# Layer 0's experts: three PSUM banks for the inner products, and gate, product, down product and copy a step or two later

## The chip, the cores and the metric

One NeuronCore of a Trainium2 chip runs the whole program. The metric is the device time of one execution in microseconds, as the median of several runs. Beside it there is one execution taken with the hardware profiler; its trace is where all rows below come from. The engines are called PE (TensorE, the matmuls), ACT (ScalarE), DVE (VectorE), POOL (GpSimd) and SP (SyncE, here only a DMA queue).

## The reference, cut to what matters

Two layers, each with cross attention and then a mixture of experts, on 32 sequences of 128 tokens of 128 features. The change touches the experts of layer 0:

```
# x: 4096 tokens (32 x 128) of 128 features, after a layer norm; 8 experts, the best 2 a token
scores = x @ Wr.T + br                       # 8 a token
idx    = top_k(scores + biases, 2);  val = softmax(scores)[idx], scaled to sum 1
h      = x @ Wl1[n] + bl1[n]                 # 128 -> 512 = a (256) and b (256)
y_n    = (silu(a) * b) @ Wl2[n] + bl2[n]     # 256 -> 128
x      = x + tanh(g_ffn[0]) * sum over the two experts of val * y_n
```

Layer 1 follows with its own attention (16 heads of 8) and experts (gelu, no gate product).

## The kernel before, in words

The whole program is one list of tasks, the plan, made by `order()` from generators that yield one step at a time. Each engine walks the same list and runs its own part of each task in that order; semaphores join the engines. So the plan's order is each engine's queue order, and a task that waits holds all that stands behind it on its engine.

For the experts the tokens are first routed: each token's row is scattered by POOL into a table in DRAM, sorted by expert, and the table is cut into blocks of 128 rows of one expert. Layer 0 has 71 blocks. `expert_steps` (L299) yields their steps. Of a block i, with the place of its tasks in the plan as it was:

- `fetch`: SP loads the block's 128 rows from DRAM, ten steps ahead.
- `turn` (step i): PE transposes the rows (L1160); ACT copies the transpose to `xb` (L1366) and copies half of the expert's weights to a ring, `block_w` (L1373); DVE computes where the results go (L1723) and copies the other half of the weights (L1735).
- `up` (step i+2): PE makes four 128x128 products into one PSUM bank (L1171); two parts are a, two are b. A product has eight records in the trace. The banks alternate, `UP_BANK` 0 and 1, so product i waits for `hidden` of block i-2. In the same task ACT makes `gate` = silu(a + bias) (L1383).
- `hide` (step i+2): DVE makes `hidden` = (b + bias) * gate (L1743), which reads the bank for the last time.
- `down` (step i+4): PE multiplies `hidden` by the second weights (L1191) into one of two other banks, and waits for the copy of block i-2 out of it. In the same task DVE adds a bias and copies the result to `y_sb` (L1758).
- `store` (step i+4): POOL scatters the 128 result rows to DRAM by an indirect DMA (L1925).

`xb` has 4 buffers, `block_w` 4, `gate` 2, `hidden` 3, `y_sb` 6. Between these tasks stand the routing of the last token group, the tables of the second part of the blocks, POOL's clears (L1871), the first keys of layer 1 (`k1`, `k_load`), and, from step 53 on, `load` and `combine`: ACT issues the load of a sequence's two results a token (L1395), and DVE adds them to `x` (L1767). `k1`, `q1` and `xt` use PSUM bank 5 (`SPLIT_BANK`), the routing of layer 0 and the bias tables bank 7 (`ROUTE_BANK`). Layer 1's attention starts in the plan at step `BLOCKS[0] + 2` of this stage, and its scores (L993) use banks 0 and 1.

Of the kernel before, what the change touches and what calls it, by code (L numbers as in the profile page):

```python
# [18 lines left out]
ACT = mybir.ActivationFunctionType  # L19
# [46 lines left out]
SPLIT_BANK = 5  # L66
UP_BANK = (0, 1)
X_BANK = (3, 2)
Y_BANK = (4, 6)
# [229 lines left out]
def expert_steps(layer, tasks, begun, after):  # L299
# [11 lines left out]
    for b in range(AMONG[layer]):  # L311
        begins = FIRST_DONE[layer] + 6 + (4 * b // 3 if layer == 0 else 11 * b // 10)
        loads.setdefault(begins, []).append(("load", layer, b))
        combines.setdefault(begins + 3, []).append(("combine", layer, b))
    begin_after = max(combines) - len(after)
    if layer == 0:
        begin_after = min(s for s in combines if ("combine", 0, GS - 1) in combines[s]) - after.index([("norm", NG)])
    for s in range(max(max(combines) + 1, n_blocks + 4)):
        step = []
        if 0 <= s - 2 < n_blocks:  # L320
            step.append(("up", first + s - 2))
# [5 lines left out]
        if s < n_blocks:  # L327
            step.append(("turn", first + s))
        if layer == 0 and 0 <= s - 2 < n_blocks:
            step.append(("hide", s - 2))  # L330
        if 0 <= s - 4 < n_blocks:
            step += [("down", first + s - 4), ("store", first + s - 4)]
        if rest:
# [23 lines left out]
def order():  # L357
# [8 lines left out]
    after0 = [[("expert", 1, e)] for e in range(NEXP)] + first_keys_and_queries()  # L366
    phases = [(attention0_steps(tasks[0]), NSEQ), (expert_steps(0, tasks[0], NSEQ + 4, after0), BLOCKS[0] + 2),
              (attention1_steps(tasks[1]), U1 + 1), (expert_steps(1, tasks[1], U1 + 5, []), BLOCKS[1])]
# [20 lines left out]
def flamingo_two_layers(nc, a, out):  # L389
# [31 lines left out]
    def xt_count(n):  # L421
        return place["xt", n] + 1
# [45 lines left out]
    with ExitStack() as stack:  # L468
# [253 lines left out]
        def blocks_of_tile(layer, b):  # L722

            return FIRST_BLOCK[layer] + (FIRST_DONE[layer] if b < GS * FIRST_GROUPS[layer] else BLOCKS[layer])

        def hiddens(n):

            return n + min(max(n, 0), BLOCKS[0])
# [181 lines left out]
        def _(pe):  # L910
            w = Waits(pe)

            def three_pass(to, wh, wl, xh, xl):
                pe.matmul(to, wh, xh, start=True, stop=False)  # L914
                pe.matmul(to, wl, xh, start=False, stop=False)
                return pe.matmul(to, wh, xl, start=False, stop=True)

            def split_task(t):
# [36 lines left out]
                elif t[0] == "q1":  # L955
                    n = NG + t[1]
                    w.wait_ge("weights1", 6)
                    w.wait_ge("split_lo", xt_count(n))
                    done = three_pass(banks[:, bank, :], w1_h[:, 0, :], w1_l[:, 0, :], xt_h[:, n % 2, :], xt_l[:, n % 2, :])
                else:  # L960
                    c0 = t[1] * GK
                    w.wait_ge("weights1", 6)
                    done = three_pass(banks[:, bank, 0:GK], w1_h[:, 1, :], w1_l[:, 1, :],
                                      ctx_th[:, c0:c0 + GK], ctx_tl[:, c0:c0 + GK])
# [81 lines left out]
            for t in plan:  # L1046
# [114 lines left out]
                elif kind == "up":  # L1161
# [5 lines left out]
                    w.wait_ge("shifted", NSEQ + layer * U1)  # L1167
                    w.wait_ge("hidden", hiddens(i - 1))
                    w.wait_ge("xb", i + 1)
                    for part in range(4 if layer == 0 else 2):  # L1170
                        done = pe.matmul(banks[:, UP_BANK[i % 2], part * P:(part + 1) * P], block_w[:, i % WR, part // 2, part % 2 * P:(part % 2 + 1) * P], xb[:, i % BR, :],  # L1171
                                         start=True, stop=True)
# [56 lines left out]
        def _(act):  # L1229
# [12 lines left out]
            for t in plan:  # L1242
# [118 lines left out]
                elif kind == "turn":  # L1361
# [5 lines left out]
                    if i < BLOCKS[0]:  # L1367
# [6 lines left out]
                                       ACT.Copy).then_inc(sem("block_w_act"))  # L1374
                elif kind == "up":
                    i = t[1]
                    layer, k, n = of_block(i)
                    w.wait_ge("up", i + 1)
                    if layer == 0:
                        w.wait_ge("hidden", hiddens(i - 1))  # L1380
                        w.wait_ge("block_bias", k + 1)
                        for half in (0, 1):
                            act.activation(gate[:, i % 2, half, :], banks[:, UP_BANK[i % 2], half * P:(half + 1) * P], ACT.Silu,  # L1383
                                           bias=block_bias[:, k, half, n:n + 1]).then_inc(sem("gate"))
                    else:
                        w.wait_ge("y_mm", i - HR + 1)
                        act.activation(hidden[:, i % HR, :, :].rearrange("p t n -> p (t n)"), banks[:, UP_BANK[i % 2], 0:HID1], ACT.Gelu).then_inc(sem("hidden"))  # L1387

# [31 lines left out]
        def _(dve):  # L1420
# [14 lines left out]
            for t in plan:  # L1435
# [300 lines left out]
                elif kind == "hide":  # L1736
# [5 lines left out]
                    for half in (0, 1):  # L1742
                        dve.scalar_tensor_tensor(hidden[:, i % HR, half, :], banks[:, UP_BANK[i % 2], (2 + half) * P:(3 + half) * P],  # L1743
                                                 block_bias[:, k, 2 + half, n:n + 1], gate[:, i % 2, half, :], ALU.add, ALU.mult).then_inc(sem("hidden"))
                elif kind == "down":
                    i = t[1]
# [208 lines left out]
```

## Time and profile before

| | us |
|---|---|
| median of 3 runs | 788.54 |
| lowest and highest | 787.5, 790.2 |
| the profiled execution's own time | 795.85 |
| its span | 794.1 |

The span runs from the first to the last instruction of the program; the execution's own time has some more around it. The profiled execution is 0.9% above the median. The products of layer 0's experts run from 247.5 to about 412 us of the span. "Idle before" in a row is time in which the engine did nothing before these instructions, and the name behind the arrow is what ended it. PE's ends are modelled, its starts are not.

### The profile page before, as it was taken

To read this page: it belongs to the slowest core of one execution; us is meant where nothing else is said; L and a number is where in the kernel's file an instruction comes from. 1 tells how busy PE (TensorE), PEld (TensorE's weight loads), DVE (VectorE), ACT (ScalarE), POOL (GpSimd) and SP (SyncE) were. 2 spreads that over 40 slices of the span, in tenths; PEclk is the share of its full clock that TensorE was granted. 3 is DMA by queue.
4 is the path that set the end of the run, shared out by engine and by line. 5 is a ranking of instruction groups with operands and counts; after the bars stand their busy time and mean duration, and the time that the engine had idled before them with its cause. 6 is when DMAs were issued, how large, how long until landed. Compare 5 with 4: busy or idle time off the path is not lost.

```text
span 794.1 us, 16522 instructions
## 1 busy us (share of the span) xinstructions
PE 647.0 (81%) x4501; PEld 584.0 (74%) x4501; DVE 556.0 (70%) x1971; ACT 442.0 (56%) x1275; POOL 448.4 (56%) x665
## 2 busy tenths in 40 slices
PE   6888888899766767978688899889879875898886
PEld 5677778888666657877677788878768874787775
DVE  3367688887874566876787889888878755444564
ACT  2476767677434434655556776767665542433452
POOL 4035357776667565875445334767656665565541
PEclk9999999998978788999997999999999996999999
DMA  9446667454422223434352435535413013332444
GB/s 261 117 115 171 174 172 182 124 154 110 127 72 87 62 79 113 110 93 119 106 156 76 114 78 107 122 85 103 113 58 84 31 34 93 102 89 79 135 145 153
DMA packets 127383, 89.48 MB, mean 113 GB/s; under 512 B 30996, under 2 KB 116276, under 8 KB 127260
## 3 DMA queue, kind: packets, MB, share of 16 engines
q1 hardware_dynamic: 110844, 64.93, 32.1%
q0 software_dynamic: 8128, 17.65, 6.8%
q10 hardware_dynamic: 8320, 5.85, 2.6%
q8 instruction: 38, 0.62, 0.3%
q14 instruction: 53, 0.43, 0.2%
HBM read 50.73 MB, written 39.85 MB: 114 GB/s over the span
## 4 chain that ended last, share of the span: by engine, by line
PE 39%; DVE 21%; issue 12%; ACT 11%; SPq 5%; another core or an unknown queue 4%; DMA 3%; POOL 2%; DVEq 1%; ACTq 0%; POOLq 0%
PE banks L1171 7%; PE banks L1191 5%; PE banks L1034 5%; SPq L824 3%; DMA v_rows<-vo 3%; DVE row_max L1428 3%; PE banks L914 2%; PE banks L1001 2%; PE banks L977 2%; PE banks L1212 2%; PE banks L1019 2%; DVE hidden L1743 2%; DVE up L1735 2%; DVE x_res L1767 2%
## 5 line engine op out<-in xcount | busy, mean ns | idle before, releaser
L1925 POOL DMA_INDIRECT y_rows<-y_sb,result_at x134 | 131.1, 978 | 107.9 <-DVE result_at L1723 46.5
L1171 PE MATMUL banks<-xb,up 128*128 128x128 f32 x820 | 127.8, 297 | 47.1 <-DVE hidden L1743 22.4
L1171 PEld LDWEIGHTS banks<-xb,up 128*128 128x128 f32 x820 | 112.8, 207 | 61.5 <-issue 33.7
L1918 POOL DMA_INDIRECT x_rows<-xm,row x120 | 120.5, 1004 | 31.6 <-issue 28.5
L1880 POOL TENSOR_TENSOR v_flat<-v_raw,row_head 104x64 f32<-104x64 f32 (+1 forms) x128 | 55.6, 461 | 73.1 <-ACT v_raw L1345 72.1
L1191 PE MATMUL banks<-down,hidden 128*128 x536 | 87.6, 289 | 8.9 <-DVE y_sb L1760 4.6
L1329 ACT ACTIVATE prob_t<-banks 128x512 f32<-128x512 f32 x192 | 73.3, 439 | 28.7 <-PE banks L1001 24.8
L1034 PE MATMUL banks<-v_flat,prob_t 128*128 128x108 f32 (+2 forms) x640 | 86.5, 284 | 3.3 <-ACT prob_t L1329 1.3
L1034 PEld LDWEIGHTS banks<-v_flat,prob_t 128*128 128x128 f32 (+1 forms) x640 | 79.7, 197 | 10.6 <-ACT prob_t L1329 6.8
L1383 ACT ACTIVATE gate<-banks,block_bias 128x128 f32<-128x128 f32 x142 | 44.4, 365 | 76.2 <-PE banks L1171 44.7
L1191 PEld LDWEIGHTS banks<-down,hidden 128*128 128x128 f32 x536 | 75.0, 202 | 12.0 <-issue 12.0
L1846 POOL TENSOR_TENSOR prob<-prob,inv_sum 128x616 f32<-128x616 f32 x32 | 39.1, 1223 | 57.8 <-DVE inv_sum L1491 57.6
L1743 DVE SCALAR_TENSOR_TENSOR hidden<-banks,block_bias,gate 128x128 f32<-128x128 f32 x142 | 42.8, 343 | 33.8 <-ACT gate L1383 27.5
L1428 DVE TENSOR_REDUCE row_max<-banks 128x8 f32<-128x616 f32 x64 | 50.4, 788 | 9.3 <-PE banks L993 9.3
L1001 PE MATMUL banks<-ident,prob 128*128 128x128 f32 (+1 forms) x375 | 56.3, 283 | 0.0
L1019 PE MATMUL banks<-vo_flat,prob_t 128*128 128x128 f32 (+1 forms) x320 | 47.4, 302 | 8.6 <-ACT prob_t L1329 6.6
L1735 DVE COPY up<-up 128x256 f32 x134 | 49.5, 370 | 6.9 <-issue 2.4
L1019 PEld LDWEIGHTS banks<-vo_flat,prob_t 128*128 128x128 f32 (+1 forms) x320 | 45.2, 217 | 9.7 <-ACT prob_t L1329 7.4
L1387 ACT ACTIVATE hidden<-banks 128x256 f32<-128x256 f32 x63 | 24.0, 382 | 45.9 <-PE banks L1171 35.8
L1760 DVE COPY y_sb<-banks 128x128 f32<-128x128 f32 x63 | 18.1, 287 | 44.5 <-PE banks L1191 32.3
L1304 ACT ACTIVATE prob<-banks,row_max 128x77 f32<-128x77 f32 x128 | 30.8, 324 | 32.7 <-issue 20.4
L1001 PEld LDWEIGHTS banks<-ident,prob 128*128 128x128 f32 (+1 forms) x375 | 46.2, 147 | 0.8 <-issue 0.2
(238 smaller groups left out, 1657.9 us busy)
## 6 DMA issues: line engine op xcount, KB each, us to landing
vo_flat<-v_rows SPq DMA_DIRECT2D x32, 256.0 KB
x_norm<-x_rows SPq DMA_DIRECT2D x74, 72.0 KB
v_rows<-vo SPq DMA_DIRECT2D x38, 128.0 KB
x_far<-x_rows SPq DMA_DIRECT2D x60, 72.0 KB
gathered<-y_rows ACTq DMA_DIRECT2D x32, 128.0 KB
q_rows<-up_raw SPq DMA_DIRECT2D x8, 512.0 KB, 2.8
q_even<-q_rows SPq DMA_DIRECT2D x12, 256.0 KB
q_odd<-q_rows SPq DMA_DIRECT2D x12, 256.0 KB
```

Of the source, the lines that this page charges most:

```text
L1001: done = pe.transpose(banks[0:chunk_rows[c], PT_BANK[k], c % 4 * SEQ:(c % 4 + 1) * SEQ], flat[:, c * P:c * P + chunk_rows[c]], ident[:, :])
L1019: done = pe.matmul(banks[:, O_BANK, 0:D], prob_t[0:rows, b % 2, c, :], vo_flat[0:rows, b % 2, c, :], start=c == 0, stop=c == CHUNKS - 1)
L1034: done = pe.matmul(banks[:, O_BANK, half * width:half * width + cols], prob_t[0:rows, u % 2, c, :], v1_flat[0:rows, first:first + cols], s ...
L1171: done = pe.matmul(banks[:, UP_BANK[i % 2], part * P:(part + 1) * P], block_w[:, i % WR, part // 2, part % 2 * P:(part % 2 + 1) * P], xb[: ...
L1191: done = pe.matmul(banks[:, Y_BANK[i % 2], 0:D], hidden[:, i % HR, half, :], of_expert(flat[:, (2 * layer + half) * D:], i, D), start=half ...
L1329: act.activation(dst, banks[0:rows, PT_BANK[k], 0:len(chunks) * SEQ], ACT.Copy).then_inc(sem("prob_t"))
L1428: dve.tensor_reduce(m_view, s_view, AX.X, ALU.max).then_inc(sem("row_max"))
L1735: dve.tensor_copy(block_w[:, i % WR, 1 - layer, :], src[:, bass.ds(at, HID1)]).then_inc(sem("block_w_dve"))
L1743: dve.scalar_tensor_tensor(hidden[:, i % HR, half, :], banks[:, UP_BANK[i % 2], (2 + half) * P:(3 + half) * P], block_bias[:, k, 2 + half, ...
L1880: pool.tensor_tensor(v1_rows[0:rows, b % 2, half, chunks[0]:chunks[-1] + 1, :, 0:DK1], v1_raw[0:rows, chunks[0]:chunks[-1] + 1, half, :, : ...
L1918: pool.indirect_dma_start(out=x_rows[layer][:, :], out_offset=bass.IndirectOffsetOnAxis(ap=row[:, n, c:c + 1], axis=0), in_=xm[:, i % 2, j ...
L1925: pool.indirect_dma_start(out=y_rows[layer][:, :], out_offset=bass.IndirectOffsetOnAxis(ap=result_at[:, i % (2 * YR):i % (2 * YR) + 1], ax ...
```

## The change

Layer 0's products go round three banks, 0, 1 and a third that is bank 5 before block 28 and bank 7 from there on. Each product waits for the last reader of its own bank. The gate gets a task of its own and stands at step i+3, ahead of that step's other tasks; `hide` stands at step i+3 (it was i+2), the down product at step i+5 (i+4), and DVE's copy, now a task `keep`, and the store at step i+6 (i+4). Loads, combines and the work of the next phase stand two steps later; the stage has two more steps of its own. The experts of layer 1 keep their order.

```diff
+UP_SWITCH = 28
-        begins = FIRST_DONE[layer] + 6 + (4 * b // 3 if layer == 0 else 11 * b // 10)
+        begins = FIRST_DONE[layer] + (8 + 4 * b // 3 if layer == 0 else 6 + 11 * b // 10)
-    for s in range(max(max(combines) + 1, n_blocks + 4)):
+    for s in range(max(max(combines) + 1, n_blocks + 6 - 2 * layer)):
         step = []
+        if layer == 0 and 0 <= s - 3 < n_blocks:
+            step.append(("gate", s - 3))
         if 0 <= s - 2 < n_blocks:
             step.append(("up", first + s - 2))
...
-        if layer == 0 and 0 <= s - 2 < n_blocks:
-            step.append(("hide", s - 2))
-        if 0 <= s - 4 < n_blocks:
-            step += [("down", first + s - 4), ("store", first + s - 4)]
+        if layer == 0:
+            if 0 <= s - 3 < n_blocks:
+                step.append(("hide", s - 3))
+            if 0 <= s - 5 < n_blocks:
+                step.append(("down", s - 5))
+            if 0 <= s - 6 < n_blocks:
+                step += [("keep", s - 6), ("store", s - 6)]
+        elif 0 <= s - 4 < n_blocks:
+            step += [("down", first + s - 4), ("keep", first + s - 4), ("store", first + s - 4)]
...
-    phases = [(attention0_steps(tasks[0]), NSEQ), (expert_steps(0, tasks[0], NSEQ + 4, after0), BLOCKS[0] + 2),
+    phases = [(attention0_steps(tasks[0]), NSEQ), (expert_steps(0, tasks[0], NSEQ + 4, after0), BLOCKS[0] + 4),
...
+        def up_bank(i):
+            if i >= BLOCKS[0]:
+                return UP_BANK[i % 2]
+            return (UP_BANK[0], UP_BANK[1], SPLIT_BANK if i < UP_SWITCH else ROUTE_BANK)[i % 3]
+        def up_before(i):
+            first = 0 if i < BLOCKS[0] else BLOCKS[0]
+            return max([j for j in range(first, i) if up_bank(j) == up_bank(i)], default=first - 1)
...
+                    w.wait_ge("hidden", 2 * UP_SWITCH)      # PE, task k1
...
-                    w.wait_ge("hidden", hiddens(i - 1))     # PE, task up
+                    w.wait_ge("hidden", hiddens(up_before(i) + 1))
+                    if up_bank(i) == SPLIT_BANK:
+                        w.wait_ge("split_lo", xt_count(NG - 1))
+                    elif up_bank(i) == ROUTE_BANK:
+                        w.wait_ge("block_bias", 2)
...
-                elif kind == "up":                          # ACT
+                elif kind == "gate":
...
-                elif kind == "down":                        # DVE
+                elif kind == "keep":
```

## Rows read from the trace of the kernel before

**Rows 1.** The page: span, busy time by engine, TensorE's granted clock in tenths.

```profile
span 794.1 us, 16522 instructions
...
PE 647.0 (81%) x4501; PEld 584.0 (74%) x4501; DVE 556.0 (70%) x1971; ACT 442.0 (56%) x1275; POOL 448.4 (56%) x665
...
PEclk9999999998978788999997999999999996999999
```

**Rows 2.** Stretches of the stage: busy us (instructions) of each engine, clock, DMA.

```profile
262.00:316.00 54.00, 39.39 (x261) 37.22 (x260) 33.45 (x147) 21.30 (x78) 29.54 (x33) 0.79 0.29 84
316.00:350.00 34.00, 29.69 (x246) 28.33 (x245) 28.08 (x91) 19.89 (x73) 27.30 (x31) 0.99 0.37 103
350.00:395.00 45.00, 32.69 (x270) 30.78 (x269) 30.58 (x125) 24.13 (x89) 22.82 (x24) 1.00 0.42 115
395.00:413.00 18.00, 16.70 (x122) 15.42 (x120) 15.34 (x58) 10.36 (x35) 8.58 (x9) 0.91 0.52 147
sum 151.00, PE 118.48 PEld 111.75 DVE 107.45 ACT 75.68 POOL 88.25; mean PE 29.62 PEld 27.94 DVE 26.86 ACT 18.92 POOL 22.06
```

**Rows 3.** Waits in 262 to 415 us: engine, line, releaser: us, times, longest.

```profile
ACT gate L1383 <- PE banks L1171: 44.7, 37, 3.4
...
PE banks L1171 <- DVE hidden L1743: 21.3, 18, 5.6
PEld banks L1171 <- ACT up L1373: 17.8, 10, 5.8
ACT gate L1383 <- remote: 13.5, 2, 8.3
...
PE banks L1191 <- DVE y_sb L1758: 4.0, 3, 1.8
```

**Rows 4.** Groups in 262 to 415 us: busy us, mean ns, idle before.

```profile
L1171 PE MATMUL banks<-xb,up 128*128 128x128 f32 x526 | 77.4, 294 | 24.9 <-DVE hidden L1743 21.3 <-issue 1.9 <-DVE up L1735 0.9
```

**Rows 5.** Timeline at full pace: start us, us, engine, line (PE only).

```profile
317.16 1.06 PE L1171 MATMUL banks<-xb,up 128*128 128x128 f32 x8
...
318.17 0.61 PE L1191 MATMUL banks<-down,hidden 128*128 x4
...
318.61 1.06 PE L1171 MATMUL banks<-xb,up 128*128 128x128 f32 x8
```

**Rows 6.** Timeline of a pause, 352 to 357 us, columns as above.

```profile
352.30 1.13 PE L1171 MATMUL banks<-xb,up 128*128 128x128 f32 x8 [0.80 <-DVE hidden L1743]
...
353.83 1.06 PE L1171 MATMUL banks<-xb,up 128*128 128x128 f32 x8
...
355.56 0.62 ACT L1383 ACTIVATE gate<-banks,block_bias 128x128 f32<-128x128 f32 x2 [2.69 <-PE banks L1171]
...
356.07 0.28 ACT L1366 ACTIVATE xb<-banks 128x128 f32<-128x128 f32 x1
356.21 0.61 DVE L1743 SCALAR_TENSOR_TENSOR hidden<-banks,block_bias,gate 128x128 f32<-128x128 f32 x2 [2.27 <-ACT gate L1383]
356.23 0.42 ACT L1373 ACTIVATE up<-up 128x256 f32 x1
...
356.53 0.63 ACT L1383 ACTIVATE gate<-banks,block_bias 128x128 f32<-128x128 f32 x2
356.75 0.29 DVE L1758 TENSOR_TENSOR y_sb<-banks,down_bias 128x128 f32<-128x128 f32 x1
...
357.08 1.13 PE L1171 MATMUL banks<-xb,up 128*128 128x128 f32 x8 [1.22 <-DVE hidden L1743]
```

**Rows 7.** Timeline of the longest hold.

```profile
288.74 0.96 POOL L1918 DMA_INDIRECT x_rows<-xm,row  x1 [0.30 <-issue]
291.30 0.62 ACT L1383 ACTIVATE gate<-banks,block_bias 128x128 f32<-128x128 f32 x2 [8.29 <-remote]
```

**Rows 8.** Timeline at the stage's end, a combine on DVE.

```profile
413.08 0.73 DVE L1767 SCALAR_TENSOR_TENSOR x_res<-gathered,token_w,x_res 128x128 f32<-128x128 f32 x2
```

**Rows 9.** Timeline early in the stage, a product at half clock.

```profile
267.40 2.05 PE L1171 MATMUL banks<-xb,up 128*128 128x128 f32 x8
```

More of the change, by code:

```diff
@@ L1167, in _ @@
                     w.wait_ge("shifted", NSEQ + layer * U1)
-                    w.wait_ge("hidden", hiddens(i - 1))
+                    w.wait_ge("hidden", hiddens(up_before(i) + 1))
[3 more added lines that the diff above has]
+                        w.wait_ge("block_bias", 2)
                     w.wait_ge("xb", i + 1)
                     for part in range(4 if layer == 0 else 2):
-                        done = pe.matmul(banks[:, UP_BANK[i % 2], part * P:(part + 1) * P], block_w[:, i % WR, part // 2, part % 2 * P:(part % 2 + 1) * P], xb[:, i % BR, :],
+                        done = pe.matmul(banks[:, up_bank(i), part * P:(part + 1) * P], block_w[:, i % WR, part // 2, part % 2 * P:(part % 2 + 1) * P], xb[:, i % BR, :],
                                          start=True, stop=True)
@@ L1374, in _ @@
                                        ACT.Copy).then_inc(sem("block_w_act"))
-                elif kind == "up":
+                elif kind == "gate":
                     i = t[1]
-                    layer, k, n = of_block(i)
+                    _, k, n = of_block(i)
                     w.wait_ge("up", i + 1)
[L1379 to L1387, printed above, removed]
+                    w.wait_ge("hidden", hiddens(i - 1))
+                    w.wait_ge("block_bias", k + 1)
+                    for half in (0, 1):
+                        act.activation(gate[:, i % 2, half, :], banks[:, up_bank(i), half * P:(half + 1) * P], ACT.Silu,
+                                       bias=block_bias[:, k, half, n:n + 1]).then_inc(sem("gate"))
+                elif kind == "up" and t[1] >= BLOCKS[0]:
+                    i = t[1]
+                    w.wait_ge("up", i + 1)
+                    w.wait_ge("y_mm", i - HR + 1)
+                    act.activation(hidden[:, i % HR, :, :].rearrange("p t n -> p (t n)"), banks[:, up_bank(i), 0:HID1], ACT.Gelu).then_inc(sem("hidden"))
                 elif kind == "load" and t[2] < AMONG[t[1]]:
@@ L1742, in _ @@
                     for half in (0, 1):
-                        dve.scalar_tensor_tensor(hidden[:, i % HR, half, :], banks[:, UP_BANK[i % 2], (2 + half) * P:(3 + half) * P],
+                        dve.scalar_tensor_tensor(hidden[:, i % HR, half, :], banks[:, up_bank(i), (2 + half) * P:(3 + half) * P],
                                                  block_bias[:, k, 2 + half, n:n + 1], gate[:, i % 2, half, :], ALU.add, ALU.mult).then_inc(sem("hidden"))
-                elif kind == "down":
+                elif kind == "keep":
                     i = t[1]
```

## The prediction

> **What bounds the kernel now.** I read the page first. TensorE (PE) is busy for 81% of the span, more than any other engine, and no engine is full [rows 1]. The change touches one stage, the experts of layer 0, so I cut it out by stretches: from 262 to 413 us PE's matmuls are busy for 118.5 of 151 us, DVE 107.5, POOL 88.3, ACT 75.7 [rows 2]. The reader is to see that PE has 32.5 us of idle time there and that it is uneven: 14.6 us in 262 to 316, 4.3 in 316 to 350, 12.3 in 350 to 395, 1.3 in 395 to 413.
>
> The waits of that stage say what the idle time is [rows 3]. PE's inner products (L1171) wait 18 times for DVE's `hidden` (21.3 us), and the load of their weights 10 times for ACT's copy of them (17.8 us); these are the same pauses, seen from two sides, so I don't add them. ACT's gates in turn wait 37 times for those very matmuls, 44.7 us. It is a ring: product of block i, gate i, hidden i, product of block i+2 in the same bank.
>
> How fast the ring could turn is seen where it is undisturbed: a block's product starts at 317.16 and the next at 318.61, so PE needs 1.45 us a block, and the down product starts 1.01 us after the product [rows 5]. Over the stage it is 2.3 us a block: 526 records of a product, eight to a block, are 66 blocks in 262 to 415 us [rows 4]. Where the rest goes is seen in one pause [rows 6]. PE records a product from 352.30 to 353.43, but its gate starts only at 355.56, 2.1 us later; the following product ended at 354.89 and its gate is the very next one. ACT was idle for 2.69 us, "<- PE". So PE's signals reach the others late and several at once. From the gate's start (call it R) the ring takes 0.65 us to `hidden` (356.21), 0.61 for that pair, and 0.26 to PE's next product at 357.08: R + 1.52. The largest such hold is 8.29 us, until 291.30; POOL's last scatter before it had ended at 289.70 [rows 7]. That is a coincidence in time, not a shown cause.
>
> **The change part by part.** It adds and removes no arithmetic: the same matmuls, gates, `hidden`, copies and stores, 71 of each. It moves them.
>
> Banks. Product i waits for `hidden` of block i-3, no longer i-2. By itself this takes `hidden` out of the ring in which PE now waits: there are three steps for it, 4.35 us at full pace.
>
> Gate and `hidden` a step later. In ACT's queue the order of a step was gate(s-2), transposed rows xb(s), weights(s); it becomes gate(s-3), xb(s), weights(s). After a hold the gate in front is now an old one, already done, so at R ACT starts with xb. In [rows 6] xb starts 0.51 after the gate and the weights 0.16 after xb, 0.42 long. Without the 0.51, weights are ready at 0.16 + 0.42 = 0.58, and PE follows at 0.58 + 0.26 = R + 0.84 in place of R + 1.52: 0.68 us saved a pause at best. This ring (transpose s, xb, weights, product s) still spans only two steps; it is what is late next.
>
> Down product and copy. Down(s-5) stands in step s and needs its bank's copy y(s-7), which `keep` makes in DVE's step s-1. Before, two steps lay between that copy and its bank's next use; now one. After a hold, xb and weights come first, the next gate starts 0.46 us later (356.53 after 356.07 [rows 6]), `hidden` 0.65 after that, the copy 0.54 after `hidden` and 0.29 long, and 0.26 to PE: R + 2.20. PE, restarted at R + 0.84, arrives there at + 1.01 = R + 1.85 and waits 0.35. So the net saving is 0.68 - 0.35 = 0.33 at worst in this arithmetic, 0.68 where the copy was early. I take 0.5, the middle. Also `hidden` of i needs down(i-3) out of its buffer; that now sits right behind product i, 0.6 us, about as long as the gate takes, so it costs 0 to 0.1 a block and is hidden by the gate.
>
> Sum: 18 pauses [rows 3] x 0.5 = 9.0 us saved. Bounds: 18 x 0.33 = 5.9, and above it all of PE's idle time.
>
> Ends. Layer 0's loads and combines, the work that comes along from the next phase (key and query loads, clears, k1), and the start of layer 1's attention all stand two steps later, with the blocks where they were. The two added steps have no product; DVE does two copies (0.29) and a combine (0.73) more between the last `hidden` and layer 1's first scores [rows 6, 8]: 1.3 us, I take 1.5 with the gather that ACT issues; 0 to 3 as bounds. The wait that k1's split now has on `hidden` of block 27 stands six steps behind it in the plan: 0. Products in bank 7 from block 28 on wait for the second bias table, copied at step 23: 0. SP's fetches keep their steps, ten blocks ahead: 0. POOL's stores come one step later on the plan (two steps after the first blocks), its queue is otherwise the same; from 316 to 350 it is busy 27.3 of 34 us with 31 instructions [rows 2], near full with the time between two issues, so nothing can be gained there, and almost nothing is lost there now (4.3 us of PE idle).
>
> Total: -9.0 + 1.5 = -7.5. The profiled execution's own time is 795.85 us (span 794.1), 0.9% above the median of 788.54; I take the difference off the median: **781.0 us**.
>
> **Two rules beside the rows.** The row says that a gate starts 2.1 us after its matmul's recorded end [rows 6]. The Trainium skill, page "Perfetto Trace Analysis", section "Tensor Engine Instruction (MATMUL, LD_WEIGHTS)", says that TensorE's end in a profile is estimated from the instruction's size, and that its semaphore is pushed once PSUM has acknowledged. By that the products could truly be running in those 2 us; then PE has nothing to give and the sum is rival C, 790, not 781.
>
> On the clock the stage is granted 1.00 from 350 to 395, although PE pauses most often there, and 0.79 from 262 to 316 [rows 2]. The skill's page "TensorE: Matmul & The Clock Gate", section "A second HAM failure mode: psum-queue depth-cycling", speaks against this change: cycling through PSUM banks gave PE small pauses between groups, in which the clock swung between its two levels. By that the time would be rival E's.
>
> **The rivals.**
> B, the pauses go almost wholly. For it: three blocks in flight cover 2 us of hold at 1.45 a block. Against: the xb ring keeps two steps. Of the 32.5 us of PE idle [rows 2] I leave 5.6, the pause behind the 8.29 us hold, and some 2: -25, plus 1.5: 765.
> C, nothing comes of it: PE is truly busy during the holds, or the holds are tied to POOL's stores, and a quicker restart only brings the next one earlier. For it: the longest hold ends behind a scatter of POOL [rows 7]. Against: at 317 the ring runs at 1.45 us [rows 5] in a stretch in which POOL, with its stores, is near full [rows 2]. Cost: the ends only, +1.5: 790.
> D, slower: the down product takes over the wait. The trace has three such waits now, 4.0 us, 1.33 each [rows 3], with two steps of slack. With one step, each block whose copy stands behind combines (0.73 each) or routing on DVE meets it: some 34 blocks in 262 to 316 and 395 to 413, a third of them at 1.33 = 15, less the 9 won, plus 1.5: +7.5, 796. It decides from the point where DVE's copy ends later than 1.01 us after the next product starts. For it: DVE is busy 15.3 of 18 us from 395 to 413 [rows 2]. Against: there PE's idle is 1.3 us at present.
> E, the clock: at 1.2 GHz the eight records of a product take 2.05 us, not 1.06 [rows 9], and a block some 1.45 more. Eight more blocks in such windows are +11.6: 800.
>
> **How the numbers follow.** Chances: forecast 0.47, B 0.17, C 0.17, D 0.14, E 0.05. The forecast's own range is 774 to 786: 2 to 15 us gained. The range of 8 in 10 reaches into B and over C: 765 to 794. A measurement tells about 0.3% (2.4 us) from no change. Faster by more: forecast and B, 0.64. Within it: C, 0.17. Slower by more: D and E, 0.19.
>
> **What would show it.** In the profile after: 350 to 395's blocks about 0.2 us shorter each; fewer and shorter waits of L1171 on `hidden`, and the remaining ones named on ACT's copy of the weights or xb; gates no longer idle for 44.7 us on PE, since they come a step later; waits of the down product on `y_sb` up from 4.0 us, but under 9. If those exceed 15 us, D holds. If PE's idle in the stage stays at 30 us with the holds as long, C. If it is under 12 us, B. Wrong altogether if the time moves in a stage that the change does not touch.

## The result and the profile after

The change makes the kernel slower: 797.48 us (median of 4 runs, 796.77 to 801.36) against 789.37 (787.5 to 793.14) on the same chip, a ratio of 1.0100 with the 95% interval [1.0062, 1.0138]. The forecast was 781.0, with a range up to 794. Repeated on a chip on which the kernel before takes 794 us, the ratio was 1.0134 [1.0100, 1.0167]; on one on which it takes 744.6 us, 1.0072 [1.0039, 1.0104].

The profiled execution of the changed kernel took 797.59 us, about its median. The one of before took 795.85, 0.9% above its own median, so the two spans can't be subtracted; I compare what happens inside the stage, and leave the totals to the timed runs.

From the page of the changed kernel, answering to [rows 1]:

```profile
span 795.8 us, 16588 instructions
...
PE 655.7 (82%) x4501; PEld 588.0 (74%) x4501; DVE 555.3 (70%) x1971; ACT 447.9 (56%) x1275; POOL 448.0 (56%) x665
...
PEclk9999999999868887999997999999999996799999
```

The stretches of the stage, answering to [rows 2]:

```profile
262.00:316.00 54.00, 40.64 (x263) 38.20 (x264) 32.17 (x147) 22.17 (x77) 28.23 (x31) 0.78 0.26 76
316.00:350.00 34.00, 29.62 (x223) 27.17 (x222) 25.56 (x86) 19.90 (x68) 24.99 (x28) 0.95 0.38 106
350.00:395.00 45.00, 38.08 (x289) 34.75 (x287) 31.48 (x126) 26.30 (x90) 23.92 (x26) 0.96 0.41 110
395.00:413.00 18.00, 14.91 (x109) 13.02 (x110) 15.04 (x56) 11.58 (x37) 8.30 (x10) 1.00 0.51 139
```

And the waits in 262 to 415 us, answering to [rows 3], with the two groups of PE that answer to [rows 4]. "Remote" stands where the profile names no instruction of this core as what ended the wait:

```profile
ACT xb L1390 <- PE banks L1180: 31.3, 24, 4.0
DVE hidden L1768 <- ACT gate L1406: 28.5, 14, 6.0
...
ACT xb L1390 <- remote: 20.2, 4, 6.8
PE banks L1215 <- DVE y_sb L1783: 17.3, 14, 4.4
...
PEld banks L1195 <- ACT up L1397: 10.3, 8, 2.4
...
PE banks L1195 <- ACT up L1397: 8.5, 5, 2.2
```

```profile
L1195 PE MATMUL banks<-xb,up 128*128 128x128 f32 x520 | 77.9, 297 | 12.8 <-ACT up L1397 8.5 <-issue 3.9
L1215 PE MATMUL banks<-down,hidden 128*128 x267 | 47.4, 304 | 17.8 <-DVE y_sb L1783 17.3 <-issue 0.2
```

L1195 is the inner product, L1215 the down product, L1180 the transpose, L1783 the copy of y. The reader is to see three things. The wait that the change aimed at is gone: the inner product's idle time fell from 24.9 us [rows 4] to 12.8, and none of it is put down to `hidden`. In its place stands a wait that was 4.0 us, three times [rows 3]: the down product waits 14 times, 17.3 us, for DVE's copy out of its bank. And ACT, which waited for inner products at its gates, now waits for transposes at its copies (31.3 and 20.2 us). Records of inner products in 262 to 415 us went from 526 to 520: the stage does not run faster. From 262 to 413 us PE is idle for 27.8 us instead of 32.5, and busy for 123.3 instead of 118.5 with slightly fewer instructions (884 for 899), so the smaller idle time is not a gain.

One such place in the timeline (start us, us, engine, line; idle before in brackets):

```profile
282.67 1.13 PE L1195 MATMUL banks<-xb,up 128*128 128x128 f32 x8
...
286.07 0.61 DVE L1768 SCALAR_TENSOR_TENSOR hidden<-banks,block_bias,gate 128x128 f32<-128x128 f32 x2 [3.77 <-remote]
286.60 0.28 DVE L1783 TENSOR_TENSOR y_sb<-banks,down_bias 128x128 f32<-128x128 f32 x1
...
287.02 1.22 PE L1215 MATMUL banks<-down,hidden 128*128 x4 [3.11 <-DVE y_sb L1783]
```

DVE's product (`hidden`) is held until 286.07. The copy is queued behind it on DVE and starts 0.53 us later; PE's down product, whose bank that copy empties, has waited 3.11 us for it. Before, that bank's copy stood one step further ahead. The three longest waits of this kind, 4.37, 3.11 and 3.18 us (down products at 262.80, 287.02 and 301.45), make 10.7 of the 17.3 us, and in each the copy starts 0.53 us behind a `hidden` that had been held for 3.8 to 6.0 us.

The same wait sits at the end of the stage, where PE goes over to layer 1's first scores (L1013):

```profile
412.12 1.13 PE L1195 MATMUL banks<-xb,up 128*128 128x128 f32 x8
413.08 0.61 PE L1215 MATMUL banks<-down,hidden 128*128 x4
414.62 0.71 PE L1215 MATMUL banks<-down,hidden 128*128 x4 [0.93 <-DVE y_sb L1783]
416.17 1.42 PE L1215 MATMUL banks<-down,hidden 128*128 x8 [0.84 <-DVE y_sb L1783]
417.34 0.53 PE L1013 MATMUL banks<-k_even,q_even 96*128 96x308 f32 x2
```

and in the kernel before:

```profile
410.52 1.13 PE L1171 MATMUL banks<-xb,up 128*128 128x128 f32 x8 [0.20 <-DVE hidden L1743]
411.48 1.29 PE L1191 MATMUL banks<-down,hidden 128*128 x8
413.10 0.52 PE L993 MATMUL banks<-k_even,q_even 96*128 96x308 f32 x2 [0.32 <-DVE hidden L1743]
```

From the start of the last inner product to the first scores: 2.58 us before, 5.22 after, 2.64 more.

### The profile page after: what moved, and what is told of

It is laid out like the page before. It is cut to its first block, busy times and chain, and to the rows that moved or that the text cites. A ratio compares the mean times of both kernels' runs of the same rounds, so it can differ in the third digit from the quotient of the medians.

```text
span 795.8 us, 16588 instructions
## 1 busy us (share of the span) xinstructions
PE 655.7 (82%) x4501; PEld 588.0 (74%) x4501; DVE 555.3 (70%) x1971; ACT 447.9 (56%) x1275; POOL 448.0 (56%) x665
## 4 chain that ended last, share of the span: by engine, by line
PE 36%; DVE 20%; issue 13%; ACT 12%; SPq 5%; DMA 4%; another core or an unknown queue 4%; POOL 4%; DVEq 1%; ACTq 0%; POOLq 0%
PE banks L1195 7%; PE banks L1215 5%; PE banks L1054 4%; SPq L843 3%; DVE row_max L1453 3%; DMA v_rows<-vo 2%; PE banks L933 2%; POOL y_rows L1950 2%; PE banks L1180 2%; PE banks L1021 2%; PE banks L997 2%; ACT prob L1328 1%; DVE prob L1456 1%; PE banks L1039 1%
## 5 line engine op out<-in xcount | busy, mean ns | idle before, releaser
L1195 PE MATMUL banks<-xb,up 128*128 128x128 f32 x820 | 129.5, 299 | 28.5 <-ACT up L1397 8.5
L1195 PEld LDWEIGHTS banks<-xb,up 128*128 128x128 f32 x820 | 114.4, 210 | 43.1 <-issue 22.2
L1215 PE MATMUL banks<-down,hidden 128*128 x536 | 92.6, 300 | 22.5 <-DVE y_sb L1783 18.1
L1215 PEld LDWEIGHTS banks<-down,hidden 128*128 128x128 f32 x536 | 77.6, 208 | 29.3 <-issue 29.1
L1390 ACT ACTIVATE xb<-banks 128x128 f32<-128x128 f32 x134 | 37.2, 278 | 72.0 <-PE banks L1180 40.6
L1785 DVE COPY y_sb<-banks 128x128 f32<-128x128 f32 x63 | 18.1, 287 | 42.4 <-PE banks L1215 26.4
```

The source lines that it names most:

```text
L1195: done = pe.matmul(banks[:, up_bank(i), part * P:(part + 1) * P], block_w[:, i % WR, part // 2, part % 2 * P:(part % 2 + 1) * P], xb[:, i ...
L1215: done = pe.matmul(banks[:, Y_BANK[i % 2], 0:D], hidden[:, i % HR, half, :], of_expert(flat[:, (2 * layer + half) * D:], i, D), start=half ...
```

## The experiments

Every ratio below is to the kernel before, on the chip of that run. "The stage" is the time in the profiled run from the end of block 0's inner product to the start of layer 1's first scores, read from the timeline. Four groups of runs came on four chips on which the kernel before takes 744 to 746 us, one group on a chip on which it takes 794. The first expectations give times for a chip with 789.4 us; only their ratios can be compared.

**The parts of the change, 744 us.** Three banks alone, every step as before (gate and product i + 2, down product and copy i + 4, tail as before):

```
-            step.append(("gate", s - 3))    # likewise hide
+            step.append(("gate", s - 2))
-                step.append(("down", s - 5))
+                step.append(("down", s - 4))
-                step += [("keep", s - 6), ("store", s - 6)]
+                step += [("keep", s - 4), ("store", s - 4)]
```

> Three PSUM banks for layer 0's products, but gate, hidden, down product, copy, store, loads and the next phase all at their old steps. Before is 789.4, the changed kernel 797.5. Theory D (the down product waits for a copy that stands one step before it instead of two): that wait stays near 4 us, the third bank costs nothing, 786 to 790. Rival T (the two steps of tail: later loads, combines and start of layer 1's attention cost the time): 787 to 790 as well, since the tail is the old one. Rival L (banks 5 and 7 themselves, or the gate's new place, cost): 793 or more if it is the banks.

Measured: 744.57 us, 1.0022 [0.9994, 1.0049]. Here the third bank by itself does nothing that can be told from zero. But this profile has no wait under "remote"; the third bank alone was not run on a chip with the late signals that it was meant to cover.

The same with the gate and product at i + 3:

```
-            step.append(("gate", s - 2))    # likewise hide
+            step.append(("gate", s - 3))
```

> Three banks, gate and hidden one step later, but down product, copy and store at step i+4 and the tail as before. Theory D: the copy keeps two steps of slack to the next use of its bank, so no gain is lost there; PE waits for hidden in the down product instead, one step behind it; 786 to 792. Rival T: 787 to 790. Rival L (the later gate costs by itself): 795 or more.

Measured: 749.00 us, 1.0059 [1.0030, 1.0088], above the kernel before, though its interval overlaps that of the third bank alone. What it adds is in its trace, 245 to 425 us: the down product, now one step behind `hidden` instead of two, waits for it.

```profile
PE banks L1215 <- DVE hidden L1768: 12.8, 14, 3.6
```

The change with the copy and the store in the down product's own step:

```
-            if 0 <= s - 6 < n_blocks:
-                step += [("keep", s - 6), ("store", s - 6)]
+            if 0 <= s - 5 < n_blocks:
+                step += [("keep", s - 5), ("store", s - 5)]
```

> The changed kernel with the copy out of the bank and the store at step i+5, beside the down product, instead of i+6; tail two steps later as in the change. Theory D: waits of the down product on y_sb fall from 18.1 us to under 6, and the time from 797.5 to 788 to 791. Rival T: the time stays at 795 to 798 though those waits are gone, since the tail is the changed kernel's.

Measured: 746.10 us, 1.0019 [0.9994, 1.0045], as theory D has it and not rival T; PE's wait for the copy is 2.0 us (3 times) from 245 to 425 us.

The change's order on two banks:

```
-            return (UP_BANK[0], UP_BANK[1], SPLIT_BANK if i < UP_SWITCH else ROUTE_BANK)[i % 3]
+            return UP_BANK[i % 2]
```

> The changed kernel's order (gate, hidden, down, copy, store and tail later) with the two old banks. Theory D: the third bank is what the later gate needs, without it PE waits for hidden of block i-2, now one step behind it: 800 to 806. Rival T: the banks don't matter, 797 to 799.

Measured: 766.73 us, 1.0319 [1.0290, 1.0348]; PE waits 21.5 us (22 times) for `hidden` from 245 to 390 us. The third bank is what the later gate needs, and on these chips it only pays that back.

**Repeats and two attempts at the order, 744 us.**

> The changed kernel as it is, on the chip of this call. The first four experiments ran where the kernel before took 744 us, not 789, and where no signal of PE came late. Theory D+H (the change adds the wait for the copy everywhere, and what it can win is only the cover of PE's late signals): where signals are prompt it is slower by more than 1%, about 1.015; where they are late about 1.010 again. Rival T (the tail of two steps): the same 1.010 on any chip.

> The kernel before as it is, for a second trace of it and for the noise: 0.998 to 1.002 of before. Where before takes 744 us every matmul's signal should follow its end within 0.1 us; where it takes 789 us gates of layer 0's experts should idle for 40 us and more again.

Measured: the change 749.00, 1.0072 [1.0039, 1.0104]; the kernel before against itself 1.0001 [0.9975, 1.0027], which is the error of the method. The change's loss is real on this chip too. Theory D+H had 1.015 here and is wrong in that: the loss is smaller where signals are prompt, not larger.

The copy put ahead of the product in DVE's step, still at i + 6:

```
-            if 0 <= s - 3 < n_blocks:
-                step.append(("hide", s - 3))
             ...
             if 0 <= s - 6 < n_blocks:
                 step += [("keep", s - 6), ("store", s - 6)]
+            if 0 <= s - 3 < n_blocks:
+                step.append(("hide", s - 3))
```

> The changed kernel, with one thing exchanged: in each step DVE copies the down product of six blocks ago out of its bank before it makes hidden, not after, so the copy no longer stands behind a gate. Theory D: PE's waits of the down product on y_sb fall from 18.1 us to under 5, and the time to 0.995 to 1.003 of before. Rival T: it stays within 0.2% of the changed kernel, as the tail is the same. Rival L (the later gate itself costs): the waits on y_sb go, but others take their place and it stays over 1.006.

Measured: 750.78, 1.0081 [1.0051, 1.0111]: nothing regained. I took this as evidence against the wait on the copy, but the wait did not go away with this order. From 245 to 425 us it is 9.5 us, against 6.7 (11 times) in the change on the same chip:

```profile
PE banks L1215 <- DVE y_sb L1783: 9.5, 16, 1.5
```

So this run does not test theory D. It also ran where no long hold stands, so what this order does to the waits of 3 to 4 us above is not known.

Gathers, combines and layer 1's first steps one step earlier:

```
-        begins = FIRST_DONE[layer] + (8 + 4 * b // 3 ...
+        begins = FIRST_DONE[layer] + (7 + 4 * b // 3 ...
-    ... expert_steps(0, tasks[0], NSEQ + 4, after0), BLOCKS[0] + 4)
+    ... expert_steps(0, tasks[0], NSEQ + 4, after0), BLOCKS[0] + 3)
```

> The changed kernel with loads, combines, the next phase's work and layer 1's attention one step earlier, so one step behind their old place and not two (two earlier would deadlock). Theory D: within 0.2% of the changed kernel. Rival T: half of the loss comes back, some 4 us.

Measured: 752.54, 1.0104 [1.0047, 1.0161], not better. Taking back one of the two added tail steps gains nothing.

**The start of the stage, 744 us.** In these profiles the first ten blocks (end of block 0's inner product to end of block 10's) took 19.4 us before and 23.0 in the change. ACT's timeline shows where. The kernel before (its repeat):

```profile
242.84 1.28 ACT L1383 ACT_TABLE_LOAD   x1
247.46 0.62 ACT L1383 ACTIVATE gate<-banks,block_bias 128x128 f32<-128x128 f32 x2 [3.33 <-PE banks L1171]
```

The change (its repeat):

```profile
248.01 0.28 ACT L1390 ACTIVATE xb<-banks 128x128 f32<-128x128 f32 x1 [4.87 <-PE banks L1180]
...
249.82 1.65 ACT L1321 ACTIVATE xm<-x_res,m_shift,m_rstd 128x128 f32<-128x128 f32 x4 [1.00 <-DVE m_shift L1558]
...
251.58 1.28 ACT L1406 ACT_TABLE_LOAD   x1
252.88 0.62 ACT L1406 ACTIVATE gate<-banks,block_bias 128x128 f32<-128x128 f32 x2
```

Gate 0, one step later, stands behind the last group's normalise (L1321), and the table load for Silu, which had filled ACT's wait for the first product, now stands in the way. First the load alone was moved back:

```
+                    if i == 1:
+                        act.activation(silu_first[:, :], zero[:, 0:1], ACT.Silu)
```

> The change, with one 128x1 Silu of a constant put behind the second block's weight copy on ACT, so that the table load for Silu (1.28 us, in the change right ahead of gate 0 at 251.58) lies in ACT's wait for the third transpose, as it did before. Theory S (the start: gate 0 came at 252.88 instead of 247.46, and the first ten blocks took 23.0 us instead of 19.4): if the load is what is late, the ratio to the kernel before falls from 1.007 by 1.3/744 to 1.005 and up 0 to up 10 takes 21.7 us. If the load only fills a wait that stands there anyway (for the normalise of the last group, 249.82), the ratio stays 1.007 and the ten blocks 23.0.

Measured: 749.25, 1.0037 [1.0016, 1.0057]; the first ten blocks took 20.1 us. The estimate is better than the change's 1.0072, but their intervals overlap.

Then the gates of the first ten blocks at their old step:

```
+        gates = [i for i in (s - 3, s - 2) if 0 <= i < n_blocks and (s - i == 2) == (i < EARLY)]
-            step.append(("gate", s - 3))    # likewise hide
+        step += [("gate", i) for i in gates]
```

> The change, but gate and product of blocks 0 to 9 stand at their old step (two steps behind the transpose's, ahead of the step's up product), those of the others a step later. Theory S (the loss of the start is the later gate behind the last group's normalise and the table load): up 0 to up 10 takes 19 to 20 us, the ratio falls from 1.007 to about 1.002. Rival (the start is slow because of the later down product and copies, or the loss only moves to blocks 10 to 20): the ten blocks take 21 us or more, or up 10 to up 34 takes 4 us more than 43, and the ratio stays at 1.006 to 1.008.

Measured: 750.95, 1.0078 [1.0045, 1.0110]. The ten blocks took 21.1 us, but the time is that of the change; where the rest went is not shown.

> The last one, and the copy and store of each block in the step of its down product (i + 5) instead of the step behind it, so that a down product waits for a copy of two steps ago. If both the start and the wait on the copy (theory D) are the loss, the gains add: 1.007 less 0.005 less 0.005 is 0.997, and the handover to layer 1's first scores is 0 to 1 us behind that of the kernel before instead of 3. If they are one loss seen twice, 1.002.

Its edit is the last one and that of the copy and store at i + 5. Measured: 744.21, 0.9973 [0.9952, 0.9994], the one kernel whose interval lies below its base. Against the run just above, on the same chip and with only the place of copy and store different, it gains 1.05% (7.8 us, 4.9 to 10.7 with both intervals); PE's wait for the copy falls from 6.7 us (12 times) to 1.5 (3 times), 245 to 425 us.

> The last one, with the gathers, the combines and layer 1's first steps one step earlier than in the change. If the two steps by which the change moves these cost time at the handover, this is 1 us (one step of 1.3 us) faster than the last, 0.996; if the gathers then wait for stores that have not landed, it is the same or 1 to 3 us slower, as it was for the change itself (1.010 against 1.007).

Its edit is the last one and the earlier tail. Measured: 747.87, 1.0004 [0.9978, 1.0030]. Its profile also shows how much one profile of the start is worth: the first blocks stand in the same order as in the last kernel and took 22.2 us, not 18.5.

**The copy or the store, 794 us.** Here the change had its full loss. The copy in its down product's step, the store left where the change has it, ten early gates:

```
+            if 0 <= s - 5 < n_blocks:
+                step.append(("keep", s - 5))
             if 0 <= s - 6 < n_blocks:
-                step += [("keep", s - 6), ("store", s - 6)]
+                step.append(("store", s - 6))
```

> Gates and products of blocks 0 to 9 at their old step, the rest a step later, every copy of y in the step of its down product (i + 5), but the store still a step later (i + 6). The kernel with copy and store both at i + 5 had the ratio 0.997, with both at i + 6 1.008. Theory D (what costs is that the next down product but one waits for the copy on DVE): the copy's place decides, 0.997 to 0.999. Rival (what costs is that the stores, and with them the gathers and y_sb's buffers, come a step later): the store's place decides, 1.005 to 1.008.

> The change itself, as the yardstick of this chip: 1.010 where the kernel before takes 789 us, 1.007 where it takes 744 us. On a chip of the first kind the three others, if the same two causes (the first blocks' gates, the copy's place) make the loss there too, stand 0.008 to 0.010 below it.

Measured: 793.53, 0.9990 [0.9963, 1.0017], against the change's 804.17, 1.0134 [1.0100, 1.0167]. The waits in 247 to 425 us of the change:

```profile
ACT xb L1390 <- PE banks L1180: 30.4, 22, 5.0
...
PE banks L1215 <- DVE y_sb L1783: 20.1, 16, 4.7
```

and with the copy at i + 5 (L1182 is the transpose, L1197 the inner and L1217 the down product, L1399 the weights' copy, L1785 the copy of y):

```profile
ACT xb L1392 <- PE banks L1182: 24.6, 22, 2.7
...
PEld banks L1197 <- ACT up L1399: 21.2, 13, 5.0
...
PE banks L1197 <- ACT up L1399: 16.5, 10, 4.8
DVE y_sb L1785 <- PE banks L1217: 12.5, 13, 1.7
```

PE's wait for the copy is down to 4.9 us (3 times); DVE now waits for the down product (12.5 us); the inner products' waits for `hidden`, which comes behind that on DVE, are 2.8 us (6 times). The stage took 160.6 us against 169.9 in both profiles of the change and 163.5 in that of before.

The gates at their old step for every block, down product, copy and store at i + 5:

```
-            step.append(("gate", s - 3))    # likewise hide
+            step.append(("gate", s - 2))
-                step += [("keep", s - 6), ("store", s - 6)]
+                step += [("keep", s - 5), ("store", s - 5)]
```

> Three banks, every gate and product of layer 0 at the old step (i + 2), down product, copy and store at i + 5: the change without its later gate and without its later copy. Against the kernel with ten early gates (0.997) it tells whether the later gate is worth anything once the first blocks are on. Theory G (a gate a step later takes 60 short waits of ACT for the product, 41 us of ACT's time, out of ACT's order, which then waits for the transposes instead, 14 to 24 us): the later gate has a small gain, this one has 1.000 to 1.002. Rival (the later gate gives nothing, the later down product with the copy in its step does it all): 0.997.

Measured: 796.36, 1.0038 [1.0013, 1.0064]; PE still waits 11.7 us (7 times) for the copy. The kernel above, with the gate later from block 10 on, had 0.9990: on this chip the later gate is worth 3.8 us (0.9 to 6.8 with both intervals), if the store's place is worth nothing.

> The kernel of ratio 0.997 (ten early gates, copy and store at i + 5) with the gathers, the combines and what hangs on them one step earlier, but layer 1's first steps where the change has them. With both earlier the ratio was 1.000. If the gathers are what collides (a gather queued on ACT before its stores have landed), this one has 1.000 as well; if it is layer 1's first steps, 0.997.

Its edit is that of the kernel of ratio 0.9973 and the first half of the tail's edit. Measured: 792.26, 0.9991 [0.9963, 1.0020]. No collision of the gathers is seen, and copy and store both at i + 5 do as well as the store a step later. As the gathers are moved too, this is no clean pair, but nothing points to the store's place as the cost.

**The copy alone, 744 us.** The edit is that of the kernel with ratio 0.9990 (`keep` at s - 5, `store` at s - 6), without its early gates:

> The change with the copy of y alone in its down product's step (i + 5), the store left at i + 6, the gates of all blocks a step later. The change had 1.0134 where the kernel before takes 794 us and 1.0072 where it takes 744; with this copy and ten early gates it had 0.999. Theory D (a down product waits for the copy, 20 us of PE's time in the change): this one takes most of it back, 1.002 to 1.004 on a 794 us chip, 1.001 to 1.003 on a 744 us chip, and PE's wait of L1215 for the copy is gone from the stage. Rival (the first blocks' gates are the greater part): 1.008 or more on a 794 us chip.

> The version that was fastest on a 744 us chip (0.9973): ten early gates, copy and store at i + 5. If it also beats the kernel before on a 794 us chip, where its kin with the store at i + 6 had 0.999, it has 0.996 to 0.999; if the gain was chance, 1.000 to 1.003.

Both came on one chip with 744.67 us before. Measured: the copy alone 744.58, 1.0010 [0.9983, 1.0038]; the repeat of the fastest version 743.85, 0.9999 [0.9971, 1.0027]. PE's wait for the copy over 245 to 390 us in the change (on its own chip, 744.60 us before), and with the copy moved:

```profile
PE banks L1215 <- DVE y_sb L1783: 6.7, 11, 1.2
```

```profile
PE banks L1217 <- DVE y_sb L1785: 1.5, 2, 0.9
```

The two waits that are left stand in the added steps at the end of the stage. The copy's place by itself takes back the change's loss there, from 1.0072 to 1.0010. What the early gates add, 0.9999 against 1.0010, can't be told from nothing, and the 0.9973 came back as 0.9999, with overlapping intervals: no version is shown to beat the kernel before.

## Why the prediction was wrong

The mechanism of the loss was on record as rival D, with 796; it had 0.14. The forecast's step that failed is the part "Down product and copy": it priced the wait for the copy at 0.35 us a pause, 6.3 us in 18 pauses, and it measured 17.3 us. The second term that failed is the net gain of 0.5 us a pause: with the copy's place undone, none of the 9.0 us is seen.

**The arithmetic of the copy.** I worked the copy out for one pause, in which ACT restarts first and the down product arrives at R + 1.85, and found 0.35 us of waiting. The timeline above shows the case that I left out: the hold sits on DVE's own product, the copy is queued behind it, and PE waits out the rest of the hold (3.11 us) instead of a third of a microsecond. The mark I had set, "if those exceed 15 us, D holds", was passed: 17.3 us in my window. The price in time: 1.0134 less 0.9990 of 794 us is 11.4 us on the slow chip (8 to 15 with both intervals), with ten early gates in it; 7.8 us (4.9 to 10.7) on one fast chip for copy and store together, all else alike; and 1.0072 less 1.0010 is 4.6 us (1.4 to 7.8) for the copy alone, between two fast chips. D's own sum had 15 for this term, but placed it in the early and last stretches because of combines and routing; most of it was in 262 to 316 (12.5 of 17.3 us, 5 waits), where the long holds are.

**The gain of 0.5 us a pause.** Undoing the copy's place should have left the 9.0 us, or more, as the 0.35 us a pause would be gone too. It left nothing: 0.9990 [0.9963, 1.0017] on the slow chip is -0.8 us with -2.9 and +1.3 as ends. On the fast chips the stage did get a little shorter with the copy moved (132.5 us for the copy alone, 132.9 and 131.9 for the fastest version, 134.0 before), but these are single profiles, the kernel with copy and store at i + 5 and every gate later took 135.7, and the timed totals show no gain that came twice. So rival C's "nothing" is, within the intervals, what the rest of the change does as a whole. That does not mean that the later gate does nothing: on the 794 us chip the kernel with every gate at its old step is 3.0 us above the kernel before (1.0038), and the later gate, from block 10 on, takes that back (3.8 us, 0.9 to 6.8). The likely reason that no more came is in the rows of the kernel with the early copy: ACT's wait for the inner product (44.7 us) has become one for the transpose, 24.6 us and 11.2 more under "remote", and PE's inner products then wait for the weights' copy behind it (16.5 us, 10 times). I had named this ring, transpose to `xb` to weights to product, as "what is late next", and gave it no price. One hold of it:

```profile
283.37 0.96 POOL L1952 DMA_INDIRECT y_rows<-y_sb,result_at  x1 [0.30 <-issue]
285.58 0.28 ACT L1392 ACTIVATE xb<-banks 128x128 f32<-128x128 f32 x1 [5.87 <-remote]
285.75 0.29 DVE L1785 TENSOR_TENSOR y_sb<-banks,down_bias 128x128 f32<-128x128 f32 x1 [3.35 <-remote]
285.98 0.42 ACT L1399 ACTIVATE up<-up 128x256 f32 x1
...
286.45 1.73 PE L1197 MATMUL banks<-xb,up 128*128 128x128 f32 x8 [4.03 <-ACT up L1399]
```

ACT and DVE, waiting for different products of PE (a transpose and a down product), are let go within 0.17 us of each other. So this hold kept back the signals of both kinds of product. It is not always one instant: in the change DVE was let go at 286.07, and ACT only at 289.01, for a transpose that PE had recorded from 280.50 to 280.77. I take it that a third bank for one kind of product can't cover such a hold while the transposes still have two. That is argued, not shown: a transpose ring of three was not tried.

**The ends.** I took +1.5 with 0 to 3 as bounds; the handover grew by 2.64 us, in the bounds. PE waits 0.93 and 0.84 us for the copy there, but the copy's later place is not the reason: with it undone the same two waits stand (1.88 and 0.62 us on the 794 us chip; 0.66 and 0.86 on a fast one), and the handover is 5.66 and 4.67 us, not 2.58. What is left is the two added steps themselves. Starting the tail a step earlier did not help.

**What the sum left out.** The start. I had costed the later gate only in the steady state. At block 0 it has other neighbours: the last normalise and a table load of 1.28 us that had been free. In the profiles the first ten blocks lost 3.6 us on the 744 us chip; in the timed runs this part is at most a few tenths of a per cent and not separated from nothing. On the chip of the prediction it is not there at all: the same ten blocks took 28.6 us before and 28.3 in the change. Why the kernel with the gate alone later had 1.0059 I can't split: it has its start (25.3 us for the first ten blocks) and the 12.8 us that its down products wait for `hidden`.

**The two rules.** The rows of the 744 us chip bear on the first. There an inner product is recorded from 378.83 for 1.13 us, and its gate starts at 380.00, 0.04 after the recorded end:

```profile
378.83 1.13 PE L1171 MATMUL banks<-xb,up 128*128 128x128 f32 x8 [0.20 <-DVE hidden L1743]
...
380.00 0.62 ACT L1383 ACTIVATE gate<-banks,block_bias 128x128 f32<-128x128 f32 x2 [1.15 <-PE banks L1171]
```

So the same instructions have no 2.1 us between end and gate there, and an error of the estimate that goes with the instruction does not explain the gap of [rows 6]. That PE's work truly ended later on the slow chips is not excluded by this; against it stands that PE started its next inner product 1.53 us after the held one [rows 6], near its full pace of 1.45 [rows 5]. The Trainium skill's "Perfetto Trace Analysis", section "Tensor Engine Instruction (MATMUL, LD_WEIGHTS)", has the end estimated, which may still be so; no run here shows it apart. The rule of the Trainium skill's "TensorE: Matmul & The Clock Gate", section "A second HAM failure mode: psum-queue depth-cycling", would have shown as a lower clock with three banks. The granted clock of the whole program was 0.933 before and 0.927 after, and on a fast chip 0.943 with three banks in the old order, where the kernel before has 0.933. In the stage, 262 to 415 us, it was 0.91 before and 0.90 after. From 316 to 395 us it fell from 0.99 and 1.00 to 0.95 and 0.96; on the fast chips the same two kernels show 0.95 before and 1.00 with the change from 316 to 350 us. So no lower clock goes with the third bank in all of these rows, and the stage as a whole lost 0.01, where E's eight blocks at the lower level would be some 0.08 (an estimate: 8 blocks of 2.9 us at half speed in 153 us). The mean of an inner product's record is 297 ns after, 294 before [rows 4].

**Marks that held.** Gates no longer wait on PE for 44.7 us (2.5 us, twice); no inner product waits on `hidden` in the window (before it one does, 3.7 us, at 253.85); what remains is named on ACT's copy of the weights; from 350 to 395 us 176 records of inner products stand where 162 stood, 2.05 us a block for 2.22, the 0.2 I had said (from 316 to 350 it is 136 for 148, the other way). All of these were right, and the time still rose: they describe the wait removed, not the end of the stage.

## What to carry to other kernels

When a step is moved away from the work it waits for, count the slack on both sides: the gate got one step more after its product, and the copy lost one of the two steps between it and its bank's next use, behind an operation that can itself be held. Price a lost step of slack by all the holds on the queue that it stands in, the long ones included, not by one short pause: here 14 waits of 1.2 us in the mean and 4.4 at most, for the 0.35 worked out from one. And before giving one ring more buffers, look whether the other rings that pass through the same engines wait in the same holds; if they do, the wait can change its name while the time stays.

## What the runs showed of the hardware

The same kernel took 744 us on some chips and 789 to 794 us on others. On the slower ones the stage has waits put down to "remote" of up to 8.3 us (18.4 us on the gates from 247 to 425 us), and in the hold shown last ACT and DVE start within 0.17 us of each other. All six profiles on the slower chips have such entries from 245 to 425 us, none of the fourteen on the faster ones has. In the kernel before on a faster chip the longest wait of a gate on PE is 3.3 us:

```profile
ACT gate L1383 <- PE banks L1171: 41.2, 60, 3.3
```

The stage took 134.0 us there, against 163.5. In the longest hold of [rows 7] and in the one shown last, POOL had indirect transfers under way when the hold began; that is again a coincidence in time, and no run took them away. The cause of the holds stays open.
